# A causal convolution with residual ahead of a GRU: all of it convolved first, or 16 steps first and the rest among the recurrent products

## What is computed

```python
# x (128, 64, 512); cond (128, 512); weights W_ih, W_hh (512, 1536); all float32
def _L0_cond_ref(x, w, b):            # depthwise causal conv over time, K = 128 taps
    y = conv_general_dilated(x, w, (1,), padding=[(K - 1, 0)], feature_group_count=D, ...)
    return y + b
def cell(h, x):
    gi = x @ W_ih + b_ih;  gh = h @ W_hh + b_hh
    r = sigmoid(i_r + h_r);  z = sigmoid(i_z + h_z);  n = tanh(i_n + r * h_n)
    h_new = (1.0 - z) * n + z * h
x = x + _L0_cond_ref(x, cond[:, None, :], conv_b)
x = x + scan(cell, cond, x over time)
```

## Time and profile before

| | us |
|---|---|
| median of three runs | 1250.97 |
| profiled execution, its span | 1249.1 |
| TensorE busy | 1207.4 |
| VectorE busy | 663.6 |
| ScalarE busy | 343.1 |
| first fp32 product of the convolution | 47.6 |
| first product of the GRU | 164.3 |

### The profile page before, as it was taken

One profiled execution on the slowest core, in us unless ns is written; L12 is line 12 of the kernel. 1 busy time (PEld: TensorE's weight loads), 2 busy tenths in 40 slices (PEclk: granted clock), 3 DMA queues, 4 the chain that ended last, 5 costly groups with the idle time before them and its releaser, 6 DMA issues.

```text
span 1249.1 us, 14699 instructions
## 1 busy us (share of the span) xinstructions
PE 1207.4 (97%) x5508; PEld 1019.2 (82%) x5508; DVE 663.6 (53%) x1015; ACT 343.1 (27%) x474; POOL 16.0 (1%) x20
## 2 busy tenths in 40 slices
PE   5499989999999999999999999999999999999998
PEld 5499978888888888888888888888888888888886
DVE  5255685555555455555555555555555555555554
ACT  6266661212212122212221211222121212122111
POOL 1000040000000000000000000000000000000000
PEclk9699999999999999999999999999999999999999
DMA  9996758222112222221222222122222211222200
GB/s 189 208 265 214 160 159 270 51 51 51 46 38 42 50 50 50 50 46 38 42 50 50 50 50 47 38 41 50 50 50 50 47 39 40 50 50 50 50 18 18
DMA packets 247730, 92.55 MB, mean 74 GB/s; under 512 B 203168, under 2 KB 236704, under 8 KB 246432
## 3 DMA queue, kind: packets, MB, share of 16 engines
q1 hardware_dynamic: 246848, 91.45, 31.9%
q10 hardware_dynamic: 864, 0.85, 0.3%
HBM read 58.72 MB, written 33.55 MB: 74 GB/s over the span
## 4 chain that ended last, share of the span: by engine, by line
PE 94%; DMA 4%; ACT 1%; POOL 0%; DVE 0%; SPq 0%; issue 0%; ACTq 0%; DVEq 0%
PE bank L715 83%; PE bank L695 9%; DMA x_sb<-in_x_dram 4%; PE bank L704 2%; ACT w_ih_hi L513 1%; ACT w_hh_hi L513 0%; POOL w_hh_lo L297 0%; DVE stage L578 0%; SPq L328 0%; DVE h_less_n L646 0%; DVE h L648 0%; DVE pre_z L640 0%; ACTq L317 0%; SPq L312 0%; ACT xT_hi L505 0%
## 5 line engine op out<-in xcount | busy, mean ns | idle before, releaser
L715 PE MATMUL bank<-w_ih_hi,xT_hi 128*128 128x512 f32 x768 | 305.5, 398 | 1.3 <-DVE w_ih_lo L297 1.1
L715 PE MATMUL bank<-w_hh_hi,hT_hi 128*128 128x512 f32 x768 | 298.9, 389 | 1.2 <-DVE w_hh_lo L297 0.8
L715 PE MATMUL bank<-w_ih_hi,xT_lo 128*128 128x512 f32 x768 | 300.0, 391 | 0.0
L715 PE MATMUL bank<-w_ih_lo,xT_hi 128*128 128x512 f32 x768 | 299.3, 390 | 0.0
L715 PE MATMUL bank<-w_hh_hi,hT_lo 128*128 128x512 f32 x768 | 298.8, 389 | 0.0
L715 PE MATMUL bank<-w_hh_lo,hT_hi 128*128 128x512 f32 x768 | 298.8, 389 | 0.0
L715 PEld LDWEIGHTS bank<-w_hh_hi,hT_hi 128*128 128x128 f32 x768 | 144.2, 188 | 31.8 <-issue 1.9
L715 PEld LDWEIGHTS bank<-w_ih_hi,xT_hi 128*128 128x128 f32 x768 | 144.3, 188 | 30.9 <-POOL w_ih_lo L297 1.0
L715 PEld LDWEIGHTS bank<-w_ih_hi,xT_lo 128*128 128x128 f32 x768 | 144.1, 188 | 31.0
L715 PEld LDWEIGHTS bank<-w_hh_hi,hT_lo 128*128 128x128 f32 x768 | 144.2, 188 | 29.9
L715 PEld LDWEIGHTS bank<-w_hh_lo,hT_hi 128*128 128x128 f32 x768 | 144.2, 188 | 29.9
(11 more groups left out here) (54 smaller groups left out, 796.6 us busy)
## 6 DMA issues: line engine op xcount, KB each, us to landing
xt<-xres SPq DMA_DIRECT2D x128, 128.0 KB, 2.6
out_dram<-out_t SPq DMA_DIRECT2D x64, 256.0 KB, 2.1
x_quads<-xres SPq DMA_DIRECT2D x252, 64.0 KB, 2.4
x_sb<-in_x_dram SPq DMA_DIRECT2D x2, 4096.0 KB, 35.3
xres<-kept SPq DMA_DIRECT2D x4, 1920.0 KB, 9.1
x_sb<-in_x_dram SPq DMA_DIRECT2D x2, 3072.0 KB, 37.8
xres<-stage SPq DMA_DIRECT2D x4, 1024.0 KB, 9.2
xres<-stage SPq DMA_DIRECT2D x2, 2048.0 KB, 8.1
```

The source lines that it names most:

```text
L715: mm = nc.tensor.matmul(psum[:, :], a[:, rows], w[which][:, cols], start=start and n == 0, stop=stop and n == 2)
```

## The change

The whole kernel is rewritten around another order of work.

- **The first 16 steps are convolved alone.** The GRU takes the last time index of the scratch tensor first (`back` = T - 1 - t), which holds step t = 0. Eight chunks of 64 channels are stacked in the partitions, 16 times each (`x_early`, eight loads of 16 partitions). Their Toeplitz blocks of 16x16 are read from a scratch tensor `kernel_full` in DRAM with a source in which each partition starts one element later (16 loads of 16 partitions, 64 B runs, on ScalarE's queue). 64 fp32 products give 16 PSUM banks, evicted to four `quarter` tiles and stored to `xres`, now [time, channel, sequence], by eight transfers of 16 partitions each.
- **Step 0's x** is computed apart: x[:, 0] transposed, times tap plus one, plus bias.
- **The other 48 steps are convolved inside the recurrence.** 256 fp32 products, one for each pair of channels with all 64 times of both, the Toeplitz tile as the stationary side and x (`x_unit`, stride 32 elements) as the moving one. Two products fill half a bank; three banks rotate. They stand on TensorE after every second or third group of three products, ten places a step in steps 1 to 13. VectorE evicts ten half banks a step.
- **Biases** are copied into the PSUM banks by ScalarE before the products, which all accumulate (`start=False`). VectorE's four bias adds go, and the sigmoids read PSUM.
- **x comes transposed** from `xres`, one load a step; the output is h transposed plus x transposed, transposed back in 32x32 blocks by VectorE, and stored by four transfers. Channels are held in an order that fits these blocks.
- The first 16 steps are unrolled on every engine.

```diff
-SLICE = 32
-PIECE = 8
+EARLY = 16
+POINTS = 10
+BULK_FIRST, BULK_LAST = 1, 13
...
         @block.sync
+            load_row(h, taps, h0_loaded)
+            load_row(x_row, x[:, 0, :], x_row_loaded)
+            for c in range(C0):
+                sp.dma_start(
+                    x_early[c * EARLY:(c + 1) * EARLY, :].rearrange("s (b g) -> s b g", g=G0),
+                    x[:, 0:EARLY, c * G0:(c + 1) * G0].rearrange("b s g -> s b g"),
+                ).then_inc(x_early_loaded, 16)
+            for w, matrix in ((0, w_ih), (1, w_hh)):
...
+            for n in range(QUARTERS):
+                sp.wait_ge(early_evicted, (n + 1) * NB0 // QUARTERS)
...
+                    sp.dma_start(xres[LATE:T, e:e + per, :].rearrange("u g b -> u (g b)"),
+                                 quarter[n][c * EARLY:(c + 1) * EARLY, :]).then_inc(early_stored[n], 16)
...
+            for n in range(QUARTERS):
+                sp.wait_ge(early_stored[n], 16 * C0)
+            load_xT(1, T - 2)
+            sp.wait_ge(early_done, NB0)
+            sp.wait_ge(k_full_stored, 16 * QUADS)
+            for b4 in range(4):
+                load_x_quarter(0, b4)
+            for j in range(T_RING):
+                load_toep(j)
+            load_xT(2, T - 3)
+            load_xT(3, T - 4)
+            for b4 in range(4):
+                load_x_quarter(1, b4)
...
         @block.scalar
+            def put_bias(psum, bias, done):
+                nc.scalar.activation(psum[:, :], bias, ACT.Copy).then_inc(done, 1)
...
             def step(i, u):
+                    act.wait_ge(xT_loaded[(u + 1) % RING], 16 * (i + 1))
                     act.wait_ge(gi_done, t + 1)
+                    nc.scalar.activation(xT_hi[:, :], xT[(u + 1) % RING][:, :], ACT.Copy).then_inc(xT_hi_ready, 1)
+                if not isinstance(i, bass.RuntimeValue) and t == 0:
+                    for n in range(QUARTERS):
+                        act.wait_ge(early_stored[n], 16 * C0)
+                act.wait_ge(gh_r_done, t + 1)
+                nc.scalar.activation(r[:, :], ps_r[:, :], ACT.Sigmoid).then_inc(r_ready, 1)
+                    put_bias(ps_r, bias_rz[:, R:R + D], bias_r_put)
...
         @block.vector
+            for n, (w, k, g) in enumerate(W_PARTS):
+                if g == R:
+                    for _ in range(2):
+                        early_evict(evicted)
+                        evicted += 1
+                if not on_pool(w, k, g):
+                    dve.wait_ge(w_hi_ready, n + 1)
+                    low_weights(nc.vector, w, k, g).then_inc(w_lo_ready, 1)
...
         @block.tensor
+            def bulk(m):
+                if m >= 3:
+                    pe.wait_ge(stage_ready, m - 2)
...
+                for pair in range(2):
...
+                    mm = nc.tensor.matmul(conv_bank[m % 3][:, pair * B:(pair + 1) * B],
+                                          toep[j % T_RING][:, slot * P:(slot + 1) * P],
+                                          x_unit[unit][:, :].rearrange("p (b g) -> p g b", g=UNIT)[:, g, :],
+                                          start=True, stop=True)
...
+                def product(psum, part_hi, part_lo, w, gate, stop, done=None):
+                    for k in range(KB):
+                        mm = block_product(psum, part_hi, part_lo, w, gate, k, stop and k == KB - 1)
+                        g = group[0]
+                        group[0] += 1
+                        if g * POINTS // GROUPS != (g + 1) * POINTS // GROUPS:
+                            bulk(bulk_bank(t, g * POINTS // GROUPS))
```

More of the change, by code:

```diff
@@ L315, in store_times, with bulk_bank @@
[L315 to L320 removed]
+        def bulk_bank(t, point):
+            if isinstance(t, int) and BULK_FIRST <= t <= BULK_LAST:
+                m = (t - BULK_FIRST) * POINTS + point
+                return m if m < NBANK else None
+            return None
@@ new lines, in conv_residual_gru, with w_cols, on_pool, number @@
+        W_PARTS = [(w, k, g) for w in range(2) for k in range(KB) for g in (R, Z, N)]
+        def w_cols(k, g):
+            return slice(k * NG + g, k * NG + g + D)
+        def on_pool(w, k, g):
+            return g == N
+        def number(w, k, g):
+            before = W_PARTS[:W_PARTS.index((w, k, g)) + 1]
+            return sum(on_pool(*part) == on_pool(w, k, g) for part in before)
+        def low_weights(eng, w, k, g):
+            cols = w_cols(k, g)
+            return eng.tensor_tensor(lo[w][:, cols], raw[w][:, cols], hi[w][:, cols].bitcast(F32), ALU.subtract)
@@ new lines, in _ @@
+            pe.wait_ge(h0_loaded, 16 * KB)
+            transpose(ps_hT, hT_done, h)
+            pe.wait_ge(x_row_loaded, 16 * KB)
+            transpose(ps_x0, x_row_done, x_row)
+            pe.wait_ge(k_full_ready, 1)
+            for psum in (ps_r, ps_z, ps_in, ps_hn):
+                mm = nc.tensor.matmul(psum[:, :], ident[:, :], k_full[:, :], start=True, stop=True)
+            mm.then_inc(banks_opened, 1)
+            pe.wait_ge(x_early_loaded, 16 * C0)
+            pe.wait_ge(y0_ready, KB)
@@ new lines, in _ @@
+            for g in range(G0):
+                n, slot = g * B // BANK, g * B % BANK
+                half, g_half = g * 2 // G0, g % (G0 // 2)
+                if g_half == 0:
+                    pe.wait_ge(toep_early_loaded[half], 16 * C0)
+                if slot == 0 and n >= 3:
+                    pe.wait_ge(early_evicted, n - 2)
+                mm = nc.tensor.matmul(conv_bank[n % 3][:, slot:slot + B], toep_early[half][:, g_half * P:(g_half + 1) * P],
+                                      x_early[:, :].rearrange("p (b g) -> p g b", g=G0)[:, g, :],
+                                      start=True, stop=True)
+                if slot + B == BANK:
+                    mm.then_inc(early_done, 1)
@@ L712, in block_product @@
+            def block_product(psum, part_hi, part_lo, w, gate, k, stop):
                 rows = slice(k * P, (k + 1) * P)
[L713 to L723 removed]
```

883 lines of the change are left out of this document (378 added, 505 removed).

## The result

The changed kernel takes 1298.02 us (median of four runs, 1296.87 to 1298.82), the kernel before 1251.57 beside it: a ratio of 1.037, 95% interval 1.0355 to 1.0385. It is slower, by 46 us. The profiled execution's span is 1296.1 us, against 1293.6 predicted and 1249.1 before.

The account below looks back on a forecast made before the run. TensorE, busy 97% of the span, was taken as the bound. Start 124.9 + steps 1050.0 + products 110 + tail 6.2 and 2.5 gave a 1293.6 us span, 1295.5 with the 1.9 offset; range 1232 to 1318.

Parts of the forecast that it names:

- The price of the product: Steps 1 to 13: each of 256 fp32 products paid in full at about 0.43 us, 110 us in all.
- The gain of the start: Before step 1: its effective begin moves from 192.9 to 124.9 us, a gain of 68.0 us.
- The rival: Fp32 products in the steps: cheap with a contiguous stationary side, 56 us instead of 110, total 1241.5; chance 0.32.
- The full price of the mixture: Rival, products among the steps: each change of matmul kind costs extra, 136 us instead of 110, total 1321.5; chance 0.11.
- x_early, 33 us: Start: eight loads of 16 partitions, 4.2 MB, take 33 us, between bounds of 19 and 39.
- The path to step 1: Start: weights in at 76.6 us, early stores at 105.6, step 1's x at 108.7; TensorE stands some 20 us.
- Step 1's begin: End of the start: step 1 at 120.9 us, before adding 1.5 for the clock and 2.5 for a stall.
- The cold clock, 1.5 us: Start: after TensorE's stand of some 20 us, a lower granted clock slows its matmuls, adding 1.5 us.
- The stall of step 1, 2.5 us: Step 1: TensorE stops by the fourth bank, step 2's x landing late; 2.5 us, bounds 0 and 12.
- Work costed at nothing: Steps: DVE evictions, ACT bias copies and bulk loads stay covered, 0 us; 64 us if cover failed by 1 a step.
- Tail: After the last matmul: the old 6.2 us plus net 2.5 for transposing and storing the last h.
- 16 partitions at 108 GB/s: Rival, start: x_early loads and early stores take 39 us each, adding 18 us, total 1313.5; chance 0.12.

Follow-up runs that it names:

- its start mended: Changed kernel with GpSimd copies, biases first, early chunks in every fourth partition, earlier loads for steps 2 and 3, weights held for early Toeplitz tiles: 1214.48 us.

## Why the prediction was right

**Direction and size.** 1295.5 was forecast and 1298.0 measured. The price of the product has its size for the reason given. The gain of the start, 68 us forecast and 70 measured, does not: two steps of its path were wrong by about 20 us each, in opposite directions. That half of the sum was luck.

- **The price of the product**: 0.43 forecast (110 us), 0.449 measured (256 x 0.449 = 115 us). The reason taken, that the strided side had only moved, is shown by four runs, one on the stationary side and three on the moving one: contiguous or 8 B apart the moving side costs 0.232 and 0.240, near the 0.22 that the transposes gave as the rival's price; 16 and 128 B apart 0.461 and 0.449. The rival named the right number for a contiguous product (1241.5; the runs with one took 1243 to 1245), but not for this one. It was argued from a price that didn't follow the clock; that price was the stride's, and the contiguous one does follow it. The allowance that a stationary load would hide under a neighbour, 0.01 a product, was wrong in sign: 0.008 more than the 0.441 of the earlier trace rows.
- **The full price of the mixture**, 136 us: excluded. Against the 0.441 of the old order, a product among the steps costs 0.008 us more, 2 us in all and not 23.
- **x_early, 33 us**: mis-sized. It was waited for until 51.4 us, so some 45 from 5.8 on, the Toeplitz transfers beside it, for which the sum had part of another 10. The lower rate was the true one, 103 to 114 GB/s from 20 us on, and transfers in flight on other groups of 16 partitions did not raise it: each took 15.0 us (the median) from issue to landing with a new one issued every 5 us or so. The last weights were there at 84.2 us, not 76.6. The Trainium skill, "SBUF — State Buffer", section "Door 1: The DMA port swizzle", gives 104 GB/s for partitions 0 to 15, which the windows bear out. Its rule, that the rate goes by which partitions are reached, agrees with the run with rows set apart (198).
- **The path to step 1**: this step failed, though its end came out right. The prediction had TensorE through step 0's h products at 92, then standing some 20 us for the load of step 1's x, until 112.3. There was no such stand: TensorE was through the h products only at 110.47, 18.5 us later than forecast, and went straight on, as step 1's x and bias were ready by 107.9. What made it late was its own work behind ScalarE's queue: the biases behind 16 Toeplitz loads, then the bank copies, the split, VectorE's order and the early products, the last of which gave way to step 0 at 93.9. None of this order was in the sum, which had 4 us for the biases' bytes and nothing for their place. The run with the biases first gave 7.6 us. The early stores, which the prediction put behind the weights (done at 105.6 us), were done at 101.8: the 128 KB stores land in some 3 us each and are held by the evictions that they wait for.
- **Step 1's begin**: 120.9 forecast; TensorE's timeline has the first h product of step 1 at 119.11. It is 1.8 us off because 18.5 us of lateness that the sum did not have stand in the place of 20.3 us of waiting that it had.
- **The cold clock, 1.5 us**: not there. TensorE was busy with the second half of the early products from 81.7 us on and went straight into step 0. And the early products had no such price either: at a granted clock of 0.50, 11 of their matmuls took 2 us, as at 0.74 (the earlier trace rows shows the same of the old ones). In the windows of TensorE:

```profile
53.00:55.00 2.00, 2.00 (x11) 0.50 1.07 265
55.00:57.00 2.00, 2.00 (x11) 0.74 1.00 252
```

- **The stall of step 1, 2.5 us**: 3.8, and by the mechanism given. This is the place where the early stores' queue counts. The load of step 2's x was issued at 126.67 behind 16 Toeplitz issues and landed at 129.75; TensorE stopped at its fourth bank, as nothing had been evicted. The chain and TensorE's waits in the changed kernel:

```profile
126.67 3.08 DMA xT<-xres
```

```profile
PE bank L637 <- DVE stage L529: 2.8, 1, 2.8
```

- **Work costed at nothing**: right. The late steps have 16.81 us as before, and in steps 1 to 13 TensorE waits for no eviction but that one.
- **Tail**: 8.7 forecast, 6.2 + 2.5. Its own terms give less: 3.65 - 1.09 is 2.5 only if the 0.7 us of the DVE add that goes is not taken off, and 1.9 with it, so 8.1. The last matmul starts at 1287.82 and ends near 1288.2, the span at 1296.1: 7.9. (the earlier trace rows has the old one.)

```profile
1287.82 0.39 PE L615 MATMUL bank<-w_hh_hi,hT_lo 128*128 128x512 f32 x1
```

By measured terms, with the old kernel's 1050.0 for the steps: 119.1 + 3.8 + 1050.0 + 115.1 + 7.9 = 1295.9, of 1296.1. The start gave 192.9 - 122.9 = 70 us, the steps took 115 and the tail 1.7.

**The rivals.** 16 partitions at 108 GB/s was the true rate of the loads, yet not the time that the rival gave, 1313.5: the early stores, 39 us of it there, were not what step 1's begin waited for, and x_early's 12 us were partly covered, as the biases bound just behind it. With x_early at 239 GB/s the kernel gains 6.6 us.

**Where the expected gain of such a change goes.** Laid between the steps, a product costs TensorE what it costs ahead of them. TensorE's 17 us of building Toeplitz matrices are gone, but 28 us of early products and 8 us ahead of them stand in their place. So the change can gain only what TensorE stood idle, 41.7 us at the most. With x read contiguously the new order is no gain by itself: it took 1243 to 1245 us, 22 more than the old order with a contiguous read, 1221.6 (there with other elements and no copy to pay for). Only with its start mended as well does it come to 1214.5, 7 below that. Neither the old order with a copy that computes the whole nor the old order with a mended start was tried, so which order is the better one with equal care stays open.

## What to carry to other kernels

Work moved in among the instructions of the engine that sets the time is paid in full, so look first at its price: here a stride of 16 B or more (16 and 128 B on the moving side, 512 B on the stationary one) about doubled an fp32 product, and a copy by an idle engine took 55 us out. To place the begin of the steady state, follow each queue in the order of its issues, small loads like biases too; what is late is often not large but behind something. Ask of every wait in a forecast what the engine would still be busy with: a late load costs nothing to an engine that is later still. A sum that comes out right can hold two wrong terms of opposite sign, so compare the landmarks one by one.

## What the runs showed of the hardware that was not expected

- The fp32 128x128x128 product takes 0.23 to 0.24 us with a moving side of 4 or 8 B from element to element and 0.45 to 0.46 with 16 or 128 B: a step, no slope. The strided price is the same at a granted clock of 0.50 and of 1.00; the contiguous one falls, from 0.22 us for a recorded matmul at 0.56 to 0.13 at 1.00.
- From 20 to 30 us, mostly packets of 256 B: 112 GB/s to 16 neighbouring partitions (103 to 114 up to 51 us), 198 to every eighth of 128, 197 and 207 to every fourth of 64, and 239 to 128 partitions.
- A transfer of 64 B packets, issued beside 32 weight transfers on another queue, landed up to 33.7 us after its issue; those issued 5 us ahead of it took 6 to 7. A bias load of 256 KB took 19 to 29 us beside the weights, and 8 to 12 where it was issued ahead of them.
- GpSimd's copies of 128x512 elements with a stride of 128 B took 1.14 to 1.22 us on the mean of a run, and VectorE's evictions beside them 420 to 422 ns (424 without).
